# Splitting the experts' weights over five pages per pair instead of four, in an attention and mixture-of-experts kernel

## What is computed

```python
x = x + _layernorm(_L0_attn_ref(_layernorm(x, axis=-1), Wq, Wk, Wv, Wo), axis=-1)
x = x + _layernorm(_L0_ffn_ref(_layernorm(x, axis=-1), gate_w, ...), axis=-1)
...
E, K, I, SI = (16, 4, 176, 704)
topk_w, topk_idx = jax.lax.top_k(routing_probs, K)
combine = (jax.nn.one_hot(topk_idx, E, dtype=x.dtype) * topk_w[..., None]).sum(1)
shared = _silu_mul(x @ shared_gate_up.T, SI) @ shared_down.T
shared = shared * jax.nn.sigmoid(x @ shared_gate_vec.T)
def step(acc, ew):
    w_gu, w_d, cw = ew
    h = _silu_mul(x @ w_gu.T, I)
    return (acc + h @ w_d.T * cw[:, None], None)
sparse, _ = jax.lax.scan(step, acc0, (expert_gate_up, expert_down, combine.T))
return (shared + sparse).reshape(orig_shape)
```

## Time and profile before

| | us |
|---|---|
| median of three runs | 626.38 |
| the profiled execution, whole | 625.45 |
| its span, from the first to the last instruction | 623.7 |
| page loop on PE, first to last gate matmul (L1938) | 415.4 to 579.8 |
| PE busy over the span | 502.3 (81%) |
| DVE busy | 414.5 (66%) |
| ACT busy | 342.6 (55%) |
| POOL busy | 325.2 (52%) |

### The profile page before, as it was taken

The page is one execution under the profiler, slowest core; times in us unless marked ns, Lnnn a source line. Parts: engine busy times, 40 slices in busy tenths (PEclk is TensorE's granted clock), DMA queues, the critical chain, the costliest instruction groups (busy, mean ns, idle before and its releaser), DMA issues.

```text
span 623.7 us, 11475 instructions
## 1 busy us (share of the span) xinstructions
PE 502.3 (81%) x3484; PEld 386.3 (62%) x3484; DVE 414.5 (66%) x1011; ACT 342.6 (55%) x701; POOL 325.2 (52%) x357
## 2 busy tenths in 40 slices
PE   2738899899999998878887783898999999999300
PEld 1614455656565453367667663787999999999300
DVE  6529878888788857259646732566997666665287
ACT  2141576696577557754442311656886666666223
POOL 5431543481464215326266575605668887777544
PEclk9859899999999999989898996898999999999755
DMA  7241651534063440340036232639998888887593
GB/s 270 66 136 51 193 185 53 166 130 152 24 212 108 128 135 2 100 141 1 18 125 227 107 108 90 204 89 267 253 250 139 147 146 148 141 129 101 79 374 143
DMA packets 71033, 86.33 MB, mean 138 GB/s; under 512 B 6272, under 2 KB 64192, under 8 KB 70976
## 3 DMA queue, kind: packets, MB, share of 16 engines
q1 hardware_dynamic: 53264, 63.15, 32.7%
q0 software_dynamic: 14448, 19.31, 17.4%
q10 hardware_dynamic: 3264, 3.15, 1.4%
HBM read 33.68 MB, written 39.12 MB: 117 GB/s over the span
## 4 chain that ended last, share of the span: by engine, by line
PE 30%; DVE 10%; issue 5%; DMA 4%; ACT 3%; another core or an unknown queue 3%; POOL 1%; ACTq 0%; POOLq 0%; SPq 0%; DVEq 0%
PE gate_ps L1938 11%; PE y_ps L1961 7%; PE y_ps L1914 3%; PE m_ps L1856 2%; PE gate_ps L938 2%; DMA acc_dram<-yout,xin 2%; DVE total L1769 2%; PE up_ps L938 1%; PE up_ps L1949 1%; PE up_ps L1950 1%; DVE hid L1665 1%; DVE ystats L1771 1%; DMA added<-acc_dram 1%; DVE hid_lo L1695 1%
## 5 line engine op out<-in xcount | busy, mean ns | idle before, releaser
L1276 POOL DMA_INDIRECT acc_dram<-yout,xin x79 | 124.5, 1576 | 59.9 <-ACT yout L1409 28.4
L702 DVE TENSOR_REDUCE nmax<-a_ps 128x2 f32<-128x768 f32 (+3 forms) x88 | 96.0, 1121 | 13.7 <-PE a_ps L837 13.2
L587 ACT ACTIVATE probs<-a_ps 128x1024 f32<-128x1024 f32 (+1 forms) x96 | 81.3, 883 | 28.4 <-PE a_ps L859 24.4
L488 POOL TENSOR_SCALAR_AFFINE_SELECT probs<-probs 128x256 f32<-128x256 f32 (+1 forms) x96 | 47.0, 500 | 91.4 <-ACT probs L587 91.3
L1264 POOL DMA_INDIRECT xs_dram<-xrow,idx x64 | 63.8, 997 | 42.1 <-issue 18.9
L1938 PE MATMUL gate_ps<-w_all,rxT_hi 128*128 x316 | 78.0, 329 | 1.3 <-issue 1.3
L1743 DVE TENSOR_TENSOR h<-rsilu,gate_ps 128x176 f32<-128x176 f32 x79 | 26.6, 337 | 50.6 <-ACT rsilu L1394 41.4
L1961 PE MATMUL y_ps<-w_all,hT_hi 128*128 x237 | 57.6, 311 | 0.7 <-DVE hT_lo L1750 0.7
L1938 PEld LDWEIGHTS gate_ps<-w_all,rxT_hi 128*128 128x128 f32 x316 | 52.5, 190 | 3.1 <-issue 2.5
L832 PE MATMUL a_ps<-KTt,QT 96*128 96x128 bf16 (+3 forms) x256 | 49.9, 305 | 4.4 <-DVE nmax L702 2.2
L1938 PE MATMUL gate_ps<-w_all,rxT_lo 128*128 x158 | 51.3, 325 | 0.0
(11 more groups left out here) (291 smaller groups left out, 1334.0 us busy)
## 6 DMA issues: line engine op xcount, KB each, us to landing
xin<-xs_dram SPq DMA_DIRECT2D x79, 136.5 KB
xs_dram<-zeros SPq DMA_DIRECT2D x7, 1365.0 KB, 6.9
w_all<-in_wex_dram SPq DMA_DIRECT2D x16, 480.0 KB
QT<-parts SPq DMA_DIRECT2D x48, 128.0 KB
KTt<-parts SPq DMA_DIRECT2D x48, 128.0 KB
acc_dram<-zeros SPq DMA_DIRECT2D x6, 640.0 KB, 8.2
added<-acc_dram ACTq DMA_DIRECT2D x12, 256.0 KB, 9.1
x_all<-in_x_dram SPq DMA_DIRECT2D x4, 512.0 KB, 8.0
```

The source lines that it names most:

```text
L488: pool.affine_select(out=pr, in_=pr, pattern=[[0, nh], [1, P]], compare_op=ALU.is_ge, fill=0.0, base=0, channel_multiplier=-1).then_inc(ma ...
L587: nc.scalar.activation(dst, src, ACT.Exp, scale=float(DH) ** -0.5).then_inc(a_act, 1)
L702: nc.vector.tensor_reduce(nmax[:, i, h:h + nh].rearrange("p (b h) -> p b h", h=hb), src, AX.X, ALU.max, negate=True).then_inc(a_dve, 1)
L1276: pool.indirect_dma_start(out=acc[a][:, :], out_offset=bass.IndirectOffsetOnAxis(ap=xin[:, p % XIN, XROW - 1:XROW].bitcast(mybir.dt.uint32 ...
```

## The change

A new helper gives for the n-th page from the first split on which expert is worked on and which piece of it: 0 the main columns, 1 the tail, and 2 for neither. Five successive pages serve two experts (main, tail, main, tail, nothing). ACT asks it with n = p-2, DVE with n = p-3. SP's loop and PE's loop are as before: the wait of SP in `expert(k)` and where it stands among the loads of rows, and the wait of PE for `w_ready`.

```diff
+        def expert_at(n):
+
+            pair, piece = divmod(n, 5)
+            return early + 2 * pair + piece // 2 % 2, piece % 2 if piece < 4 else 2
...
-                if p >= 2 and early + (p - 2) // 2 < E:
-                    if p % 2 == 0:
-                        expert_high(early + (p - 2) // 2)
-                    else:
-                        expert_tail_high(early + (p - 2) // 2)
+                k, piece = expert_at(p - 2)
+                if early <= k < E:
+                    if piece == 0:
+                        expert_high(k)
+                    elif piece == 1:
+                        expert_tail_high(k)
...
-                if p >= 3 and early + (p - 3) // 2 < E:
-                    if p % 2 == 1:
-                        expert_low(early + (p - 3) // 2)
-                    else:
-                        expert_tail_low(early + (p - 3) // 2)
+                k, piece = expert_at(p - 3)
+                if early <= k < E:
+                    if piece == 0:
+                        expert_low(k)
+                    elif piece == 1:
+                        expert_tail_low(k)
```

## The result

| | before | after |
|---|---|---|
| median of 6 runs, us | 626.36 (625.57 to 630.11) | 633.46 (631.00 to 638.77) |
| profiled execution, us | 625.45 | 633.47 |
| its span, us | 623.7 | 631.7 |

The ratio is 1.0109, with an interval of 1.0070 to 1.0148: 6.8 us slower, 4.8 us above the forecast of 628.7 and above the upper end of the range, 632.2. It lies at the bound of 1% that divides "the same" from "slower", with the interval on both sides of it.

What follows compares the result with a forecast made beforehand. PE's matmuls in the page loop were taken as the bound, with 1.75 us at most to regain. The sum -1.3 - 0.2 + 1.9 + 1.9 = +2.3 us gave 628.7 us; own range 627 to 630, 8 in 10 within 624.8 to 632.2.

Steps and rivals of the forecast that it cites:

- Late rows: At turn_in(24), iteration 22, PE waits for page 24's rows, queued behind SP's `w_ready` wait and rank 14's load: +1.9 us.
- waits at pages before 22: A sign that the prediction is wrong altogether: waits appearing in the page loop ahead of page 22.
- The last expert: Ahead of gate(30) PE waits for rank 15, which DVE now finishes on page 29: +1.9 us, bounds 1.0 and 2.4.
- What is given back: Mostly between gate(21) and gate(29), PE regains time from freer neighbours: -1.3 and -0.2 us, at most 1.75.
- ACT's two waits: ACT's stands for the loads of ranks 14 and 15, 0.60 and 0.93 us, go away: -1.3 us.
- a freer DVE: DVE gets 10 us of pace for work that had 8: -0.2 us, bounds 0 and -0.47.
- The rows did not come in time: Rival: rows come in time, the wait in iteration 22 falls to 0 to 0.5 us; 626.2 us, chance 0.22.
- The convoy on SP: Rival: rank 14's load takes 7.3 us, PE idles 4.7 us in iteration 22 and loses the clock; 633.0 us, chance 0.08.
- The granted clock: Rival: the clock falls in both new waits, costing 1.5 us each; 631.7 us, chance 0.12.

Runs made afterwards that it cites:

- s9_rows_first: Changed kernel with SP issuing the rows of two more pages ahead of the `w_ready` wait and load from rank 8 on; third batch: 613.60 us, ratio 1.0057.
- e9_rows_first: Changed kernel with SP issuing the rows of two more pages ahead of the `w_ready` wait and load from rank 8 on; second batch: 612.33 us, ratio 1.0010.
- e6_last_late: Kernel before with rank 15 alone split late, ACT on pages 27 and 28, DVE on 28 and 29; 614.50 us, ratio 1.0061.
- e12_thin_low: Kernel before with DVE's main subtraction cut to 64 of 960 columns for ranks 5 to 15; 627.09 us, ratio 0.9996.
- e14_small_after: Changed kernel with the main load of ranks 5 to 15 cut to 64 of 960 columns, engine work kept; 628.32 us, ratio 1.0025.
- r_before: Kernel before, unedited, run again on another chip in the second batch; 611.34 us, ratio 0.9998.
- u_before: Kernel before, unedited, run again in the fifth batch; 627.21 us, ratio 1.0005.
- e13_small_before: Kernel before with the main load of ranks 5 to 15 cut to 64 of 960 columns, engine work kept; 623.74 us, ratio 0.9936.
- t_after: Changed kernel, unedited, run again in the fourth batch; 630.72 us, ratio 1.0054.
- e1_sp_pattern: Changed kernel with SP issuing expert loads by the same five-page pattern in place of every second page; 615.70 us, ratio 1.0095.
- e2_last_early: Changed kernel with the last expert, rank 15, split one page earlier on ACT and DVE; first batch: 613.22 us, ratio 1.0053.
- s2_last_early: Changed kernel with the last expert, rank 15, split one page earlier; third batch: 612.88 us, ratio 1.0042.
- e3_both: Changed kernel with SP's loads by the five-page pattern and rank 15 split one page earlier; 610.57 us, ratio 1.0006.
- e10_rows_last: Changed kernel with rows of two more pages ahead of the load from rank 8 on and rank 15 split one page earlier; 609.98 us, ratio 1.0002.
- s_after: Changed kernel, unedited, run again in the third batch; 614.42 us, ratio 1.0065.

## Why the prediction was right in its waits and wrong in its time

**Late rows: right in the main.** Forecast +1.9 at turn_in(24) with nothing beside it; measured 1.38 + 0.71 in the first profile, 1.82, 2.34 and 2.37 at turn_in(24) in the three others, each with 0.4 to 0.6 us at turn_in(22) or turn_in(20), where the prediction had something left over. It had named waits at pages before 22 as a sign of being wrong, and in three of four profiles they came, though small. That the stand of SP for `w_ready` makes the rows late is read from the timelines of SP, DVE and PE, and putting the rows ahead of it removes every such wait in `s9_rows_first`. It doesn't in `e9_rows_first`, the same kernel, where SP's wait for ring slots took its place (1.37 us at turn_in(24)). Nor does a wait there need the change: two profiles of edits with the old order of SP have it too, 1.38 in `e6_last_late` and 1.00 in `e12_thin_low`, while the three profiles of the kernel before have none. The Trainium skill (DMA: Bandwidth & Descriptors, "Queues, rings and completion order") says that on each DMA engine the descriptors of SP's row are consumed in ring order, though a later one may finish its write before an earlier one. The trace agrees with that order: page 24's rows could be used 4.3 us after their issue behind rank 14's load of 608 KB, and 3.1 us behind the load of 160 KB in `e14_small_after`.

**The last expert: right.** Forecast +1.9, measured 1.72, 1.74, 1.95 and 1.97; gone in the kernels that finish rank 15 a page earlier, and 2.00 in the kernel before when rank 15 alone is moved.

**What is given back: wrong.** This is the step that failed: -1.3 for ACT's two waits and -0.2 for a freer DVE. ACT's waits did go, and DVE did become freer, and the loop outside its waits grew by 0.6 us in the first pair of profiles. Over four profiles of the changed kernel, with its waits and the loss by the clock taken off, pages 8 to 32 are 49.9 to 50.8 us (mean 50.2); in three of the kernel before they are 49.4, 50.2 and 51.7 (mean 50.4). So about 0.2 us was given back and not 1.5. Three things stand against the step. First, the 1.28 us between gate(21) and gate(29) came from one execution: in `r_before` there was 0.5 to give back there, in `u_before` 2.6 (18.73 us). Second, the work on DVE is worth little: cutting most of its main part (`e12_thin_low`) bought some 0.9 us in the profile, on pages 15 and 23, and nothing that shows in the median, while cutting the bytes (`e13_small_before`), and with them ACT's waits for loads, bought about 4 us of the median. Third, the new order has small losses of its own that I had not counted, and they eat up what a freer DVE gives (page 23 took 1.99 to 2.12 us in the four profiles of the changed kernel, 0.4 to 0.7 less than before). From page 8 to 21 it took 27.65 us against 26.65. Page 12 took 2.18 us, 0.2 too long, and did so in every profile of the changed kernel (2.18 to 2.23), while it took 1.99 in every one of the kernel before. DVE's rows there:

```profile
446.07 0.18 DVE L1736 TENSOR_TENSOR picked<-xin,onehot 128x32 f32<-128x32 f32 x1
...
446.39 1.15 DVE L1652 TENSOR_TENSOR w_all<-w_all 128x960 fp32r<-128x960 f32 x1
447.45 0.33 DVE L1749 TENSOR_TENSOR h<-rsilu,gate_ps 128x176 f32<-128x176 f32 x1
...
448.15 0.41 DVE L1756 TENSOR_TENSOR hT_lo<-up_ps,hT_hi 128x256 fp32r<-128x256 f32 x1
```

The main subtraction now falls on a page that also has the selection. I had worked out those 2.58 us and used them only to date `w_ready` for ranks 11 and 15, never as a delay of PE; on any such page DVE falls behind a pace of 2.0, and `hT_lo` ended at 448.56, with PE's y matmuls behind it at 448.70. In pages 18 and 20 (2.31 each) this can't be separated from the rows in the first profile. But page 20 took 2.19 and 2.18 in `s9_rows_first` and `e14_small_after`, which have the new order and no wait for rows there, against 1.99 in all three profiles of the kernel before.

With the give-back at zero the same sum would have been about +3.8, 630.2 us, still 3.3 below the measured 633.5. The three later pairs of the changed kernel came out 2.4, 4.5 and 3.2 us slower, and +3.8 lies among them, while the forecast's +2.3 is just below the smallest; all are inside the stated range taken relative to the kernel before (-1.6 to +5.8).

**The first ratio.** The 6.8 us of the first measurement are larger than those three and above the range. Of the 8.0 us of its profiled execution 4.5 are the change's stretch, with much the same length as in the other profiles of it on pages 8 to 32 (54.56, 54.87, and 56.62 with the fallen clock). The other 3.3 lie where the programs don't differ. Other profiles differ there by as much. Pages 2 to 8 took 17.37, 17.05 and 17.64 us in three executions of the kernel before, and 18.48, 16.52, 17.05 and 16.38 in four of the changed one, so the first profile has the longest of all seven. Ahead of that, gate(2) started anywhere between 415.9 and 422.2 us in the six later profiles of the slower measurements, in kernels that are all alike up to there. That makes spread of few runs the likely cause of this part. It isn't shown for the median of the first measurement, for which there is one profile only. The range had room for the bounds of the mechanisms but none for this spread, and that was its fault.

**The rivals.** The rows did not come in time (this rival counts two fifths fewer splits per page, but five pages in place of four are one fifth fewer). The convoy on SP (7.3 us to land) did not come in the first profile: 5.2 us from the load's issue to the use of the rows. The granted clock stayed at 1.00 behind both waits in three of four profiles; in `t_after` it fell, at 1.6 us for a price of 1.5 forecast. It fell in three profiles of edited kernels as well, behind 2.22 us (`e1_sp_pattern`, at 2.8 us), 2.47 (`e2_last_early`) and 2.53 (`s2_last_early`, about 1.5 us each). So this rival was sized well and isn't rare. The Trainium skill (TensorE: Matmul & The Clock Gate, "HAM oscillation") warns that a wait for a DMA between bursts of matmuls can throttle the clock. The traces agree in part: of 19 waits of PE of 1.3 us or more on pages 8 to 32, in all profiles of this case together, the granted clock fell behind four, the two longest among them, and stayed at 1.00 behind 2.34 and 2.37 us.

**What stays open.** Why `e14_small_after` stands 4.6 us behind `e13_small_before` in the medians when its two waits are 2.4 and the profiles differ by 3.4 on pages 8 to 32, and how often SP's wait for ring slots, not the one for `w_ready`, is what holds the rows. The versions without either wait equal the kernel before (`e3_both` 1.0006, `e10_rows_last` 1.0002), as does the one shifted by two pages (0.9989); none of these beats it.

## What to carry to other kernels

When a step is slowed that releases a wait of an in-order queue, count how many steps lie between that release and the first use of anything queued behind it; the busy shares don't show that slack running out, and this count gave the two large waits to about half a microsecond each. Count every wait of that queue: here it had a second one, for ring slots, which took over where the first was removed. Don't credit work taken off the engines beside the bottleneck, nor waits for loads seen in one execution only: here both together gave back some 0.2 us of 1.5. A cost of half a per cent wants a pair of kernels on more than one chip, since the same pair gave 1.0109, 1.0044, 1.0065 and 1.0054.

## What the runs showed of the hardware

Measurements of the same kernel differ by 16 us from chip to chip: medians of the kernel before were 626.4, 627.5 and 628.2 us in three measurements and 610.7, 611.3 and 610.0 in three others, while pages 32 to 78 took 93.0 to 93.4 us everywhere. In the profiles of the slower ones the chain of waits ahead of the page loop has stalls without a releaser of its own, as in the kernel before:

```profile
337.47 5.74 another core or an unknown queue
...
370.91 11.60 issue
```

The profile doesn't tell what they are; the faster profiles (`r_before`, `s_after`) have none over 2.5 us between 310 and 390 us.

The wait at turn_in(24) did not vanish with the bytes of the load ahead of the rows: with one fifteenth of its columns it was still 0.67 us (`e14_small_after`), where it is 1.4 to 2.4 us with all of them. So the late issue and the large load in front each have a part in it.
